# A macaron block on one core: the outer feed-forward layers rebuilt, and the order of every engine written anew

## What is computed

```
x = x + 0.5 * ffn(layernorm(x), w_up, w_down)          # input FFN
x = x + layers(layernorm(x), ...)                      # 8 layers
x = x + 0.5 * ffn(layernorm(x), w_up, w_down)          # output FFN, same weights

def ternary_linear(x, w):      # w_t = -1, 0 or 1 by |w| > 0.5 * mean|w|
    rms = sqrt(sum(x * x, -1)) / sqrt(d)
    return (x / (rms + 1e-8)) @ w_t.T
ffn(x) = ternary_linear(gelu_erf(ternary_linear(x, w_up)), w_down)     # 128 -> 512 -> 128

# one of the 8 layers
Q = elu(x @ Wq + bq) + 1;  K = elu(x @ Wk + bk) + 1;  value = x @ Wv + bv
KV = sum_s(K * value);  Ksum = sum_s(K);  V = Q * KV / (Q * Ksum + 1e-6)
x = ln(gelu_tanh(V @ Wo + bo) + x)
x = ln(gelu_tanh(gelu_tanh(x @ W1 + b1) @ W2 + b2) + x)
```

## Time and profile before

| | us |
|---|---|
| median of 3 runs | 959.16 (956.42 to 959.33) |
| the profiled execution | 957.2 |
| its span, first to last instruction | 955.4 |
| PE / DVE / ACT / POOL busy | 868.9 / 870.9 / 832.9 / 515.1 |
| ACT's share of the chain that ended last | 73% |

### The profile page before, as it was taken

One profiled execution on the slowest core, in us unless ns is written; L12 is line 12 of the kernel. 1 busy time (PEld: TensorE's weight loads), 2 busy tenths in 40 slices (PEclk: granted clock), 3 DMA queues, 4 the chain that ended last, 5 costly groups with the idle time before them and its releaser, 6 DMA issues.

```text
span 955.4 us, 14548 instructions
## 1 busy us (share of the span) xinstructions
PE 868.9 (91%) x3915; PEld 595.7 (62%) x3915; DVE 870.9 (91%) x3421; ACT 832.9 (87%) x1214; POOL 515.1 (54%) x617
## 2 busy tenths in 40 slices
PE   3986579999999999999999999999999999995887
PEld 2876336666666666666666666666666666553787
DVE  6999669999999999999999999999999999967883
ACT  2754679999999999999999999999999999983653
POOL 4887413555555545555555555455445544554774
PEclk9999679999999999999999999999999999996998
DMA  5000000000000000000000000000000000000011
GB/s 156 1 2 1 25 9 1 1 15 21 1 1 15 21 1 1 15 21 0 1 14 21 1 15 1 20 0 15 1 12 1 1 1 1 0 1 1 12 34 46
DMA packets 19520, 12.07 MB, mean 13 GB/s; under 512 B 1160, under 2 KB 18288, under 8 KB 19440
## 3 DMA queue, kind: packets, MB, share of 16 engines
q1 hardware_dynamic: 19440, 11.13, 4.1%
HBM read 9.03 MB, written 2.10 MB: 12 GB/s over the span
## 4 chain that ended last, share of the span: by engine, by line
ACT 73%; DVE 8%; POOL 7%; PE 6%; issue 5%; DMA 0%; POOLq 0%; SPq 0%; DVEq 0%; ACTq 0%
ACT h L656 16%; ACT x_fm L671 9%; ACT L656 8%; ACT rec L633 6%; ACT rec L642 4%; ACT L679 4%; ACT L697 4%; ACT e_k L623 4%; ACT e_k L616 4%; ACT bank L649 4%; ACT bank L663 3%; ACT e_q L623 3%; ACT e_q L616 2%; DVE z L779 2%; PE bank L368 2%
## 5 line engine op out<-in xcount | busy, mean ns | idle before, releaser
L1167 POOL TENSOR_TENSOR x_lo<-x_fm,x_hi 128x512 fp32r<-128x512 f32 x128 | 172.4, 1347 | 257.3 <-DVE x_hi L932 257.3
L456 PE MATMUL bank<-h,w 128*128 128x512 f32 x512 | 261.1, 593 | 0.5 <-ACT h L656 0.5
L779 DVE TENSOR_SCALAR z<-bank,mv,rstd 128x128 f32<-128x128 f32 x512 | 171.9, 402 | 17.3 <-POOL rstd L1159 17.1
L656 ACT ACTIVATE h<-bank,par 128x512 f32<-128x512 f32 x256 | 170.6, 696 | 1.5 <-PE bank L376 0.6
L374 PE MATMUL bank<-x_hi,w_hi 128*128 128x512 f32 x256 | 159.7, 624 | 13.2 <-ACT h L656 10.2
L1159 POOL TENSOR_TENSOR rstd<-ve,minus_half 128x4 f32<-128x4 f32 x128 | 139.7, 1092 | 10.7
L456 PEld LDWEIGHTS bank<-h,w 128*128 128x128 f32 x512 | 91.7, 190 | 31.5 <-issue 16.5
L765 DVE BATCH_NORM_STATS2 st<-bank 128x6 f32<-128x128 f32 x512 | 111.2, 278 | 0.0
L374 PE MATMUL bank<-x_hi,wqkv_hi 128*128 128x512 f32 x192 | 97.0, 505 | 9.6 <-DVE phi_k L850 7.2
L671 ACT ACTIVATE x_fm<-bank,par 128x512 f32<-128x512 f32 x128 | 97.8, 789 | 7.3 <-PE bank L368 7.3
L376 PE MATMUL bank<-x_hi,w_lo 128*128 128x512 f32 x256 | 101.4, 396 | 0.0
(11 more groups left out here) (105 smaller groups left out, 1924.7 us busy)
## 6 DMA issues: line engine op xcount, KB each, us to landing
x_tm<-in_x SPq DMA_DIRECT2D x8, 256.0 KB, 3.9
raw_w<-in_W SPq DMA_DIRECT2D x8, 256.0 KB, 2.7
w<-in_W SPq DMA_DIRECT2D x8, 256.0 KB, 2.9
out<-x_tm SPq DMA_DIRECT2D x8, 256.0 KB, 2.3
raw_qkv<-in_Wk SPq DMA_DIRECT2D x8, 64.0 KB, 2.5
raw_qkv<-in_Wq SPq DMA_DIRECT2D x8, 64.0 KB, 2.3
raw_qkv<-in_Wv SPq DMA_DIRECT2D x8, 64.0 KB, 2.2
wo<-in_Wo SPq DMA_DIRECT2D x8, 64.0 KB, 2.5
```

The source lines that it names most:

```text
L456: mm = pe.matmul(m.ps_o[:, :], m.w2[T.weights][:, c, :], m.h[:, T.par, c, :], start=c == 0, stop=c == FC - 1)
L656: act.activation(m.h[:, T.par, c, :], m.ps_h[c % 2][:, :], ACT.Gelu_apprx_tanh, bias=column(m, B1, T.layer, c, FC)).then_inc(s.gelu_h[T.pa ...
L779: last = dve.tensor_scalar(dst[:, j, :], src(j), mv[:, j, 0:1], scale[:, j:j + 1], ALU.subtract, ALU.mult)
L1167: pool.tensor_tensor(m.x_lo[:, T.slot, :], m.x_fm[:, T.slot, :], m.x_hi[:, T.slot, :].bitcast(F32), ALU.subtract).then_inc(done, 1)
```

## The change

Three groups of edits. The engines' lists are all rewritten.

**Outer FFN.** `normal` moves from DVE to ACT. The powers are of var+eps and var (both 0.5) instead of one of each sign; three small DVE operations follow instead of four, and beta takes two instead of three. The three POOL adds become one DVE add, 128x1024, and PE sums the two remaining parts (eight one-column matmuls instead of four). The Gelus write a buffer of their own (m.fh), hsq is single, the down product always uses bank o, in two halves; squares use bank q.

```diff
-        pool.tensor_tensor(total, sq[:, 0, :], sq[:, 1, :], ALU.add).then_inc(f.part_sums, 1)
...
-        pool.tensor_tensor(total, total, sq[:, 3, :], ALU.add).then_inc(f.hss, 1)
+    def add_squares(F):
...
+        dve.tensor_tensor(m.hss[:, F.par, :, :], m.hsq[:, 0:2, :], m.hsq[:, 2:4, :], ALU.add).then_inc(F.f.hss, 1)
+    def squares(F):
...
+        for j in range(BLK):
             for i in range(2):
+                last = pe.matmul(m.ps_q[:, j:j + 1], m.hss[:, F.par, i, j * P:(j + 1) * P], m.ones[:, 0:1],
+                                 start=i == 0, stop=i == 1)
+    def normal(F):
...
+        for j in range(BLK):
+            last = act.activation(m.fz[:, F.par, j, :], m.x_tm[:, F.t, j, :], ACT.Identity,
+                                  bias=sc[:, SHIFT, j:j + 1], scale=sc[:, ALPHA, j:j + 1])
+        dve.scalar_tensor_tensor(sc[:, DEN, :], sc[:, SD_EPS, :], EPS_RMS, sc[:, SD, :], ALU.mult,
+                                 ALU.add).then_inc(F.f.den, 1)
```

```diff
+TICKS_IN = NT // 2
+FIRST_TICK, END_TICK = -31, 74
+    def l(k, lag):
         job = 2 * (tick - lag) + k
+    def a(k, lag):
+        t = 2 * (tick - lag + TICKS_IN) + k
+        return Outer(f[0], t) if 0 <= t < NT else None
+    def b(k, lag):
+        t = 2 * (tick - lag - TICKS) + k
+        return Outer(f[1], t) if 0 <= t < NT else None
```

**Table sets and small things in the layers.** The table of Exp and Ln is loaded only where the set in use is another:

```diff
+def load_exp_and_ln(act, tables):
+    if tables["now"] != EXP_AND_LN:
+        act.preload_act_table_set(EXP_AND_LN)
+    tables["now"] = EXP_AND_LN
```

More of the change, by code:

```diff
@@ L478, in tensor_tick @@
[L478 to L491, removed]
@@ L507, in tensor_tick @@
[L507 to L516, removed]
-            return
[L518 to L523, removed]
-            return
[L525 to L528, removed]
-            for i in range(2):
[L530 to L534, removed]
-            return
[L536 to L581, removed]
-            down(tick - 2)
-        else:
-            up(tick - 5, 2)
-            turn(tick - 4)
-            up(tick - 5, 3)
-            down(tick - 6)
-            up(tick - 4, 0)
-            up(tick - 4, 1)
-            squares(tick - 6)
-            enter(tick - 0)
@@ L647, in gelu_o @@
             return
+        tables["now"] = ACT.Gelu_apprx_tanh
         act.wait_ge(s.proj_o, T.n)
@@ new lines, in outer_residual, with stats_c @@
+    def outer_residual(F):
+        if not F:
+            return
+        dve.wait_ge(F.f.beta, F.n)
+        dve.wait_ge(F.f.down, F.n)
+        for j in range(BLK):
+            last = dve.scalar_tensor_tensor(m.x_tm[:, F.t, j, :], m.ps_o[:, j * P:(j + 1) * P],
+                                            m.scale[:, F.par, BETA, j:j + 1], m.x_tm[:, F.t, j, :], ALU.mult, ALU.add)
+        last.then_inc(F.f.x_new, 1)
+    def stats_c(F):
+        if not F:
+            return
+        dve.wait_ge(F.f.x_new, F.n)
+        at_least(dve, F.f.mv_c, F.n - 2)
+        block_stats(dve, token_source(F), m.fst_c[:, F.par], F.f.stats_c)
@@ new lines, in vector_tick @@
+    stats_c(a(0, -23))
+    stats(l(0, 3), 1)
+    sum_kv(l(1, 1))
+    var_eps_c(a(0, -22))
+    z_lo(b(1, 37))
+    var_eps(a(0, -26))
+    add_squares(a(0, -24))
+    var_eps_c(a(1, -22))
+    beta(a(1, -23))
+    outer_residual(a(1, -23))
+    outer_stats(b(0, 35))
+    z_lo(a(0, -25))
+    stats_c(a(1, -23))
+    mean_square(a(0, -24))
+    round_k(l(0, 0))
+    outer_stats(a(1, -26))
+    z_c(a(0, -22))
+    means(l(0, 3), 1)
+    mean_v(l(0, 1))
+    phi_k(l(0, 0))
+    alpha(b(1, 36))
+    z(l(1, 2), 0)
@@ new lines, in vector_tick @@
+    add_squares(a(1, -24))
+    beta(a(0, -24))
+    z(l(0, 3), 1)
+    neg_ksum(l(1, 1))
+    sum_kv(l(0, 0))
+    outer_residual(a(0, -24))
+    attend(l(0, 1))
+    residual(l(1, 3), 1)
+    mean_square(b(1, 38))
+    outer_stats(a(0, -27))
+    over_ksum(l(1, 1))
+    sum_value(l(1, 1))
+    beta(b(1, 38))
+    mean_v(l(1, 1))
+    alpha(a(0, -26))
+    round_q(l(0, 0))
+    outer_means(b(0, 35))
+    sum_value(l(0, 0))
+    mean_square(a(1, -24))
+    hi(l(1, 2), 0)
+    attend(l(1, 1))
+    residual(l(0, 1), 0)
@@ L1102, in gpsimd_engine @@
+    neg_ksum(l(0, 0))
+    z(l(0, 1), 0)
+    over_ksum(l(0, 0))
+    hi(l(0, 3), 1)
+    z(l(1, 3), 1)
+    phi_k(l(1, 0))
+    outer_means(b(1, 35))
+    beta(b(0, 37))
+    residual(l(1, 1), 0)
+    residual(l(0, 2), 1)
+    round_q(l(1, 0))
+    alpha(a(1, -26))
+    var_eps(b(1, 35))
+    hi(l(1, 3), 1)
+    hi(l(0, 1), 0)
+    stats(l(1, 1), 0)
+    phi_q(l(1, 0))
+    means_c(a(1, -23))
+    means(l(1, 1), 0)
+    outer_residual(b(0, 37))
+    alpha(b(0, 35))
 def gpsimd_engine(pool, m, s, f):
```

851 lines of the change are left out of this document (463 added, 388 removed).

## The result

The changed kernel takes 962.90 us (median of 8 runs, 959.03 to 964.09); the kernel before, on the same chip, 958.43 (8 runs, 956.42 to 959.89). The ratio is 1.0040, with a 95% interval from 1.0026 to 1.0055: slower by 0.4%, where 934 us were forecast.

What follows compares the result with a forecast made beforehand. ACT was taken to bound the full ticks, busy 661.8 of 665.2 us, with the tick unchanged at 22.93 us. The sum was 957.2 - 13 - 3 - 7 - 0.4 = 933.8, so 934 us, range 916 to 951.

Steps and rivals of the forecast that it cites:

- the layers' ends: Fill and drain of the layers: 12 fewer table loads, 11 counted at 14.1 us; 13 us gained in all, bounds 0 to 22.
- the input FFN: First stage: PE and partners pace at 7.9 us a tile, last down stays at 87, shorter tail; 3 us gained (0 to 9).
- the output FFN: Last stage: 77.5 us from first enter to DVE's last residual where it was 84.4; 7 us gained (3 to 11).
- the 0.4 of `hi`: Last layer step: leaving `hi` out of the last layer gives 0.4 us.
- So I take 22.93 us: Layers' full ticks: the new lists of ACT, PE and DVE fit the present tick of 22.93 us, so nothing gained.
- Rival 1: Layers' full ticks lengthen: by 1 us, 965 us and slower, chance 0.07; by 0.1 to 0.7, 937 to 955, chance 0.16.
- My sum for the drain: Layers' drain: 33 to 34 us from the last reciprocal, where 46.2 are needed now; ACT idle 13 us, where it was 10.7.
- rival 3: Layers' ends: the removed loads lie in waits, last job's chain sets the drain; 3 us gained, not 13, 944 us; chance 0.1.
- about where it does: Input FFN: the first down product keeps its place at 28 us.
- Rival 2: Both FFNs: large DVE add and POOL powers wait for each other, up to 1 us per add; 944 us; chance 0.12.

Runs made afterwards that it cites:

- e1: Changed kernel with DVE's phi_q and residual of the even tile put ahead of attend of the odd tile: 949.14 us, ratio to the kernel before 0.9908.
- e12: Changed kernel, own DVE order, with the one POOL x_lo that runs beside attend cut to half its columns: 948.09 us, ratio to the kernel before 0.9906.
- e4: Kernel before with only the table loads made conditional, so the 12 loads of the partial ticks go: 958.06 us, ratio 0.9996.
- e9: Changed kernel with the four operations of normal in both outer FFNs back on DVE, behind shift: 969.63 us.
- e2: Changed kernel with a second DVE add of 512 columns in place of four of PE's one-column square matmuls per tile: 966.07 us.
- e5: Changed kernel with a second DVE add for four square matmuls, plus an earlier Square, z_lo ahead of the residual, output FFN squares later on PE: 966.00 us.
- e6: Changed kernel with PE's squares over only one of the two parts of hss, leaving out half the sum of squares: 954.35 us.
- C: The changed kernel itself, with the whole change against the kernel before: 962.90 us, ratio 1.0040.
- e11: Changed kernel with the DVE order of e1, POOL's input FFN x_lo one pair behind x_hi, and the Gelu table loaded before the first normal: 947.30 us.

## Why the prediction was wrong

Of the 25 us between the forecast and the profiled execution 9.5 lie in the full ticks, 7.7 at the layers' ends, 3.9 in the input FFN and 4 in the output FFN with the 0.4 of `hi`. The first alone turned a gain into a loss.

**The full tick: wrong, and it decides the sign.** The step that failed is "So I take 22.93 us", the one I called thin cover: I laid DVE's list against the clock with each operation at its own time and let `attend` of the odd tile take 0.6 us (the prediction doesn't print this row of the layout). Rival 1 even named Wo, `attend` and x_lo, but priced them by ACT's busy share before, where the same stall had slack behind it. The row to look at was not the stall's length, which I had (1.0 us), but what stands behind it in the new list and who waits for that: the residual, and PE with 98% of its round used. It gave +0.35 us a tick, 9.5 us over the full stage, within the part of rival 1 that I gave 0.16. Without it the change makes the kernel faster: e1 and e12 are at 948 to 949, still 14 to 15 us above the 934.

**The layers' ends: 5.3 us for 13. The count was right, the worth was wrong.** From the first K projection to the first full tick are 49.7 us for 53.2, from the drain's load to the last copy 46.7 for 48.5. 126 loads, 14.1 us off ACT's work; e4 shows 0.0 us off the time (0.9987 to 1.0005). My sum for the drain followed ACT's remaining work and the last job's chain, and left out PE's list. In e1's trace PE goes on from the last reciprocal, at about 822.3, until 857.3 with two gaps of 0.8 us, because the up and down steps of the last jobs come late in its list; the last layer norm ends 9.2 us later, at 866.5. That is 44.2 us; ACT has one load in it, at 822.93, and waits 21 us for PE. That PE's list holds the stretch up to 857.3 is read from this trace; no run has another list of PE there. It is nearest to rival 3, to which I gave 0.1: the loads did lie in waits, but more than the last job's chain made them. Where e1 is faster than before between first K and the last copy, 761.0 for 766.9, about 2 us of it are ticks and the rest lies at the ends, so something in the new orders there is worth about 4 us; which part wasn't tried.

**Input FFN: +0.9 for -3.** Squares, add and `normal` cost what I said (1.7, 1.23 and 1.6 us), and PE paces the stage (55.52 of 55.52 us). The first down product did not come "about where it does", at 28, but at 33.8: the first transposes come 1.2 us later (18.68 for 17.47), the list puts an up chunk and the squares ahead of the down that stood behind it before (2.3 us), and PE waits for two Gelus (2.0 us). The downs then take 55.5 us, not 59, so the last one ends 2.5 us later, where I had put it at the old place. From there to the first K projection are 12.9 us for 14.5: 1.6 less and not 3, since the last z_c is stretched by 3.8 us, not 2.5. Of the 1.2 us at the first transposes 0.6 are `normal` on ACT (from DVE's last small operation to the transposes 2.1 us for 1.5), the rest a later start of DVE's statistics (12.61 for 11.94). e9 has the 1.5 back and starts its downs no earlier, for another wait, so it doesn't tell how much of the late start is `normal`'s doing. How much better another order could start the stage stays open.

**Output FFN: -3.4 for -7.** The first down at 20.8 us and the tail are as forecast; from the first down to the last are 58.9 us for 55.9. I had subtracted too much for what lies ahead of the first one: PE works in between with one gap of 0.3 us, so it is PE work that I didn't count.

**Rival 2** (the large add waits for powers, or powers for it) fell by its price: 16 adds of 1.22 us mean, none held up. Two powers were held up by an add (1.90 us at 45.52, 2.06 at 60.18, for 1.01), but PE is busy there without a gap. The sum, with the measured terms against the profiled execution before: 957.2 + 0.9 + 4.3 - 3.4 = 959.0.

## What to carry to other kernels

When an order is rewritten, list the instructions that another engine is known to hold up, and look in the new list at what stands directly behind each: the same 1 us stall costs nothing ahead of slack and 0.35 us a round ahead of the operand of the next engine. Time taken off the busiest engine in a fill or drain is worth what the other engines' lists allow there: lay all four out, not the one with the largest share. And where an engine runs without a gap, leaving it more work can cost less than the wait that comes in its place: e2 and e5 took 0.85 us of matmuls a tile off PE, and both were 3 us slower.

## What the runs showed of the hardware

- **Who holds whom.** In these traces a POOL TENSOR_TENSOR over SBUF tiles holds up a DVE TENSOR_SCALAR over SBUF until it ends: the two instructions of `attend` take 1.63 us beside an x_lo of 512 columns, 1.09 beside one of 256, and 0.61 alone. DVE operations with a PSUM operand beside the same x_lo keep their time (0.74 and 0.68 us in e1). A DVE add that starts inside a POOL power isn't held (74.96 in a power from 74.50, and 81.22 in one from 81.18: 1.23 us each), but a power that starts inside the add takes twice its time, here and at 60.18 (2.06 us):

```profile
44.55 1.01 POOL L1300 TENSOR_TENSOR scale<-scale,plus_half 128x4 f32<-128x4 f32 x1 [0.63 <-DVE scale L1043]
45.52 1.90 POOL L1300 TENSOR_TENSOR scale<-fmv,plus_half 128x4 f32<-128x4 f32 x1
```

  The add ran from 45.33 to 46.56. The Trainium skill (SBUF — State Buffer, SBUF: two separate sides) has an exclusive lock that whoever starts first keeps for the whole instruction; the second case fits it and the first doesn't.

- **The granted clock behind a gap.** Behind some waits of PE in the FFNs the granted clock is at 1.2 GHz: in e2 behind 1.00 us (the down product at 69.96), in e6 behind 1.51 us (at 943.53). Behind others it isn't: in the kernel before 32 down matmuls take 3.84 us behind a wait of 2.03 us (82.95 in the earlier trace rows), as they do without one. So the length of the wait alone doesn't tell it. It also falls near PE's waits at the start of the input FFN, at other times in other executions, though C and e1 have the same lists there. The window from 32 to 38 us in C's profile, then in e1's:

```profile
32.00:38.00 6.00, 6.00 (x51) 5.82 (x51) 3.13 (x9) 4.19 (x7) 1.01 (x1) 1.00 0.01 3
```

```profile
32.00:38.00 6.00, 6.00 (x26) 5.71 (x27) 2.83 (x9) 3.41 (x6) 1.01 (x1) 0.50 0.01 3
...
103.00:152.00 49.00, 35.88 (x109) 22.88 (x109) 31.75 (x128) 39.61 (x58) 18.32 (x29) 0.79 0.06 17
```

  PE does 26 matmul records for 51 in the same 6 us. e1's first K projection is 2.4 us later than C's, and its fill, at 0.79 for 0.87, 2 us longer: 4.4 us together, which is what lies between e1's profiled run (951.71) and its fastest (947.33), and about what lies between C's profiled execution and its median. e12's profiled execution (952.43, its fastest 947.00) has the clock at 1.2 GHz from 32.2 us on too, and e11's (947.30) has 1.00 in that window. That the cause is the same in C is inferred; no execution of C near the median was profiled.
